# Cross-attention: the blocked values built by VectorE behind the subtraction of maxima, in place of GpSimd

## The reference

```python
ci = rms_norm(hidden_states, ln_post_cross_w)
cq = heads(ci @ cq_w, NH, CHD)                  # NH = 16 heads, CHD = 8
ck, cv = jnp.split(encoder_outputs @ ckv_w, 2, axis=-1)
ck, cv = (heads(ck, NH, CHD), heads(cv, NH, CHD))
cctx = sdpa(cq, ck, cv, causal=False)           # softmax(q k^T / sqrt(8)) v
cctx = cctx.transpose(0, 2, 1, 3).reshape(b, l, CC)
hidden_states = hidden_states + cctx @ cdense_w
```

## Time and profile before

| what | value |
|---|---|
| device time, median of 3 runs | 2231.86 us (2225.55 to 2236.3) |
| device time of the profiled execution | 2225.6 us |
| its span | 2223.8 us, 62412 instructions |
| granted TensorE clock, mean over the span | 0.967 |
| the two cross-attention phases in the span | 488.4 to 638.8 us and 1827.5 to 1977.0 us |

### The profile page before, as it was taken

The page is one execution under the profiler, slowest core; times in us unless marked ns, Lnnn a source line. Parts: engine busy times, 40 slices in busy tenths (PEclk is TensorE's granted clock), DMA queues, the critical chain, the costliest instruction groups (busy, mean ns, idle before and its releaser), DMA issues.

```text
span 2223.8 us, 62412 instructions
## 1 busy us (share of the span) xinstructions
PE 2066.6 (93%) x23424; PEld 1669.0 (75%) x23425; DVE 1368.3 (62%) x2791; ACT 1139.9 (51%) x2603; POOL 853.1 (38%) x1109
## 2 busy tenths in 40 slices
PE   7988898879979998999999979999999979979998
PEld 5656676656659997788888868897777756659997
DVE  6776776757763333666666655554788867763343
ACT  4764555438853333445444534545566637863332
POOL 1655554438942221111111112222544428952222
PEclk9999999989989998999999999999999999989999
DMA  7426877734032112200000010002444424011111
GB/s 237 122 90 140 108 118 127 104 43 111 33 99 68 57 59 72 73 2 2 2 2 2 2 42 20 19 24 92 139 134 134 126 47 124 33 49 58 58 59 34
DMA packets 122751, 159.21 MB, mean 72 GB/s; under 512 B 40867, under 2 KB 99056, under 8 KB 122384
## 3 DMA queue, kind: packets, MB, share of 16 engines
q1 hardware_dynamic: 104720, 99.59, 15.6%
q0 software_dynamic: 16560, 55.23, 11.9%
q10 hardware_dynamic: 1232, 1.05, 0.2%
HBM read 86.69 MB, written 56.28 MB: 64 GB/s over the span
## 4 chain that ended last, share of the span: by engine, by line
PE 79%; DVE 7%; issue 3%; DMA 2%; ACT 1%; POOL 1%; another core or an unknown queue 0%; POOLq 0%; DVEq 0%; ACTq 0%; SPq 0%
PE ps_all L2477 4%; PE ps_all L2479 4%; PE ps_all L2478 4%; PE ps_all L1717 3%; PE ps_all L1689 3%; PE ps_all L1242 3%; PE ps_all L1228 3%; PE ps_all L1260 3%; PE ps_all L2051 2%; PE ps_all L2502 2%; PE ps_all L2504 2%; PE ps_all L2503 2%; PE ps_all L2487 2%; PE ps_all L1703 2%; PE ps_all L1676 2%
## 5 line engine op out<-in xcount | busy, mean ns | idle before, releaser
L410 POOL TENSOR_TENSOR a_probs<-a_probs,a_sm 128x1024 f32<-128x1024 f32 x32 | 60.9, 1903 | 346.8 <-DVE a_sm L405 346.8
L1436 POOL TENSOR_TENSOR pool_w<-s_qkt,const 128x512 f32<-128x512 f32 x128 | 131.4, 1048 | 105.6 <-ACT s_qkt L1364 98.3
L2477 PE MATMUL ps_all<-f_wh,f_xh 128*128 x396 | 153.7, 388 | 5.3 <-DVE f_xl L2623 5.3
L2183 ACT ACTIVATE self_w<-ps_all,a_q_bias 128x256 f32<-128x256 f32 x128 | 53.7, 471 | 184.7 <-PE ps_all L2027 184.7
L2479 PE MATMUL ps_all<-f_wl,f_xh 128*128 x396 | 148.0, 374 | 0.0
L2478 PE MATMUL ps_all<-f_wh,f_xl 128*128 x396 | 148.0, 374 | 0.0
L2618 DVE SCALAR_TENSOR_TENSOR f_h<-ps_all,rstd,f_act_g 128x688 f32<-128x688 f32 x66 | 61.7, 934 | 135.1 <-PE ps_all L2479 135.1
L1832 POOL TENSOR_TENSOR c_kx<-kv_k,const 128x512 f32<-128x512 f32 x128 | 131.3, 1051 | 3.9 <-PE ps_all L1689 2.3
L381 DVE TENSOR_REDUCE s_mx<-ps_all 128x8 f32<-128x512 f32 x128 | 82.5, 686 | 76.4 <-PE ps_all L1228 69.1
L2541 ACT ACTIVATE f_act_g<-ps_all,rstd 128x688 f32<-128x688 f32 x66 | 55.2, 837 | 134.7 <-PE ps_all L2479 134.7
L2502 PE MATMUL ps_all<-f_dh,f_hh 128*128 x396 | 118.3, 299 | 3.9 <-DVE f_hl L2633 3.9
(11 more groups left out here) (342 smaller groups left out, 6921.6 us busy)
## 6 DMA issues: line engine op xcount, KB each, us to landing
qkv_sorted<-pool_w SPq DMA_DIRECT2D x66, 392.0 KB, 4.3
pool_w<-pool_w SPq DMA_DIRECT2D x128, 68.0 KB
s_x_in<-x_sorted SPq DMA_DIRECT2D x66, 128.0 KB
f_x_in<-x_sorted SPq DMA_DIRECT2D x66, 128.0 KB, 2.0
x_res<-x_sorted SPq DMA_DIRECT2D x66, 128.0 KB, 2.1
x_sorted<-x_res POOLq DMA_DIRECT2D x1, 4224.0 KB, 17.3
l_rows<-in_x SPq DMA_DIRECT2D x32, 128.0 KB, 2.3
x_res<-in_x SPq DMA_DIRECT2D x32, 128.0 KB, 2.9
```

The costliest lines, as they stand in the source:

```text
L1436: ins = nc.gpsimd.tensor_tensor(kx[:, p % 2, c], qkt[:, p % 2, 2 + c].rearrange("p (b k) -> p b k", b=2).unsqueeze(2) .broadcast_to([P, 2, ...
L2477: nc.tensor.matmul(bank, x_high, wh[:, w_at], start=(c == 0), stop=False)
```

## The change

`v_blocks` moves from the POOL program to the DVE program. The instruction and its waits are the same, issued on the other engine. In the DVE loop it stands behind `front(p)` and ahead of `residual(p-2)`, and it builds pair p, where GpSimd built pair p+1 in the same turn. The POOL loop keeps `spread`, `rstd_` and `put_sorted`.

```diff
                     spread(0)
                     spread(1)
-                    v_blocks(0)
                     rstd_(0)
                     for p in range(PAIRS + 3):
                         if has(p + 2):
                             spread(p + 2)
-                        if has(p + 1):
-                            v_blocks(p + 1)
                         if has(p) and p % G == G - 1 and has(p + 1):
                             rstd_(p // G + 1)
...
+                    def v_blocks(p):
+
+                        for (g0, _), c in zip(VALS, vals_in):
+                            if p == g0 * G:
+                                dve.wait_ge(c.handle, c.at(4))
+                        if pv_pe.due(p - 1):
+                            dve.wait_ge(pv_pe.handle, pv_pe.at(p - 1))
+                        nc.vector.tensor_tensor(
+                            vb[:, p % 2, :, :, :, 0:CHD].rearrange("p b j h d -> p (b j) h d"),
+                            v_all[:, p].rearrange("p b (j d) -> p (b j) d", d=CHD).unsqueeze(2)
+                            .broadcast_to([P, 2 * J, 2, CHD]),
+                            const[:, C_HALF:C_HALF + 2].unsqueeze(1).unsqueeze(3).broadcast_to([P, 2 * J, 2, CHD]),
+                            ALU.mult).then_inc(v_ok.handle, 1)
+
...
                     for p in range(PAIRS + 2):
                         if has(p):
                             front(p)
+                        if has(p):
+                            v_blocks(p)
                         if has(p - 2):
                             residual(p - 2)
```

More of the change, by code:

```diff
@@ L1836, in spread @@
                         ins.then_inc(kx_ok.handle, 1)
-                    def v_blocks(p):
-                        for (g0, _), c in zip(VALS, vals_in):
-                            if p == g0 * G:
-                                pool.wait_ge(c.handle, c.at(4))
-                        if pv_pe.due(p - 1):
-                            pool.wait_ge(pv_pe.handle, pv_pe.at(p - 1))
-                        nc.gpsimd.tensor_tensor(
-                            vb[:, p % 2, :, :, :, 0:CHD].rearrange("p b j h d -> p (b j) h d"),
-                            v_all[:, p].rearrange("p b (j d) -> p (b j) d", d=CHD).unsqueeze(2)
-                            .broadcast_to([P, 2 * J, 2, CHD]),
-                            const[:, C_HALF:C_HALF + 2].unsqueeze(1).unsqueeze(3).broadcast_to([P, 2 * J, 2, CHD]),
-                            ALU.mult).then_inc(v_ok.handle, 1)
                     def rstd_(g):
```

## The result

| | before | after |
|---|---|---|
| device time, median of 4 runs each | 2230.32 us (2225.55 to 2236.3) | 2265.64 us (2255.28 to 2271.98) |
| after / before | | 1.015, 95% interval 1.0109 to 1.0192 |
| profiled execution | 2225.6 us | 2266.34 us (span 2264.5) |
| first to last scores, cross-attention 1 and 2 | 132.96 and 132.83 us | 147.03 and 148.83 us |

The change makes the kernel slower by 35 us, 1.5%, where the prediction said +5 us and at most +16. The forecast was wrong; the slower rival (GpSimd keeps the port through both halves of a spread, 2253) was right in its mechanism and still 13 us short.

The account below looks back on a forecast made before the run. PE was taken to set the turn. Removed GpSimd work 0, undisturbed cost 0, port collisions 14 x 0.2 to 14 x 0.5 (3 to 7 us), taken as 5: 2231.9 + 5 = 2237 us, range 2228 to 2248.

Parts of the forecast that it names:

- What bounds the kernel, and the 39 us off GpSimd: Cross-attention: PE sets the turn; nobody waits for the 64 instructions leaving POOL, 39 us, worth nothing by themselves.
- Undisturbed cost 0: DVE turn: the added instruction takes 0.42 us, pushes the residual by 0.34, and costs PE nothing.
- Exclusion, and its price by `b - arrival - 0.55`: `v_blocks` against a running spread: whoever comes second waits for the other's instruction; PE pays b - arrival - 0.55, if positive.
- allowance of 0.42: DVE path to `out_t`: blocked values may be about 0.42 us late (0.16 + 0.25) before PE pays.
- The places: Group ends: blocked values arrive 0.02 us from the spreads' start; seven group ends per phase, 14 in both.
- a waiting DVE gets in between two spreads: Back-to-back spreads on GpSimd: DVE waits for one only, b = 516.01, cost 0.52 us.
- durations near 2.2: DVE durations in the changed kernel's profile: named as the sign of GpSimd keeping the port through both halves.
- VectorE is first: Tie at a group end: the spread waits 0.3, DVE nothing; 0.2 to 0.25 us in four turns, 3 us in sum.
- rival of both halves: Spreads at group ends: GpSimd keeps the port throughout, 1.53 us once in four turns, 21 us, 2253; chance 0.15.

Follow-up runs that it names:

- e1: Changed kernel with `v_blocks` on VectorE as two one-input reductions over a length-one axis, into blocks zeroed once; 2240.25 us, ratio 1.0016.
- e4: Changed kernel with the product by the mask as two `tensor_scalar` instructions of 128x128, one mask column each; 2258.0 us, before beside it 2235.6.
- e2: Changed kernel with GpSimd's indirect DMA issued ahead of the group's `rstd_` instead of behind it; 2236.09 us, ratio 1.0021.
- e3: Changed kernel with GpSimd's indirect DMA issued between the two halves of each spread; 2236.2 us, before beside it 2235.6.
- e7: Changed kernel with each half of a spread as two GpSimd instructions of 128x256; 2245.3 us, before beside it 2234.6.
- e11: Changed kernel with each spread as eight GpSimd instructions of 128x128; 2250.4 us, before beside it 2237.7.
- e9: Changed kernel with a GpSimd power of 128x4 replacing the indirect DMA issue ahead of the spread, that DMA issued behind the spread; 2266.5 us, before beside it 2237.7.
- e6: Changed kernel with a 128x1 memset on GpSimd ahead of the spread in every fourth turn; 2266.8 us, before beside it 2234.6.
- e12: e1 with three VectorE reductions of 128x512 behind `v_blocks` in every fourth turn; 2272.9 us, before beside it 2246.2.

## Why the prediction was wrong, point by point

- **What bounds the kernel, and the 39 us off GpSimd: right.** e1 takes the same 39 us off it and its turns stay at 4.25.
- **Undisturbed cost 0: right.** L1912 takes 0.41, from the rope product's 0.42. The idle time ahead of the reciprocal went down from 0.43 to 0.10 us, as forecast, and the maxima's idle of 0.42 stays:

```profile
516.52 0.41 DVE L1921 TENSOR_TENSOR x_res<-ps_all,x_res 128x256 f32<-128x256 f32 x1
517.04 0.26 DVE L1897 RECIPROCAL c_inv<-ps_all 128x16 f32<-128x16 f32 x1
```

- **Exclusion, and its price by `b - arrival - 0.55`: right.** b is the end of the GpSimd instruction that is waited for; `v_blocks` as the product of two tensors ends 0.28 to 0.29 behind it (the tensor_scalar of e4 0.10). With the b that the traces show, the formula gives for after 526.78 - 524.70 - 0.55 = 1.53 (measured 1.51), for e2 0.27 (0.24), for e3 0.45 (0.42), for e7 1.29 (1.26), for e11 1.65 (1.62). All lie within 0.03 us, so the allowance of 0.42 that is in this formula was right too.
- **The places: right.** Seven group ends a phase, 14 in all, with the asking 0.02 to 0.08 us before the spread. The turn behind loses nothing: L1912 takes 0.45 to 0.48 there, well inside the allowance.
- **The step that failed is "a waiting DVE gets in between two spreads".** From it came b = 516.01 and a cost of 0.52 us in four turns; it should have been 517.02, and the runs showed VectorE shut out through both halves, L1912 at 2.37 to 2.43 us and 1.51 to 1.56 us lost in four turns at full clock. The sign that the prediction had named for this, durations near 2.2, is what the trace shows. The row behind it, the scaling of the earlier trace rows, stood behind a spread with no DMA issue ahead of it, and the spread of the earlier trace rows follows an issue, 513.87 + 1.06 = 514.93, by 0.03. e9 shows that this is a difference, for instructions of 128x512. The prediction doubted its row for VectorE's number of elements, which isn't what mattered (e4 has as many as that row and is shut out).
- **"VectorE is first" (3 us) did not happen.** By start times VectorE was 0.02 to 0.08 us ahead of the spread in after, 0.05 to 0.11 in e6 and 0.18 to 0.24 in e9, and lost each time; in e11 it was 0.07 to 0.24 ahead eight times and won. The Trainium skill (SBUF — State Buffer, section "SBUF: two separate sides") lets the first to start have the pair for its instruction. Counted against the spread alone, the measurement says otherwise in after, e6 and e9 and agrees in e11. But VectorE asked while the DMA issue ahead of the spread was still under way, at most 0.23 us before its end, or within 0.01 us behind it. In e11 the six wins at 0.13 us ahead and more took 0.47 to 0.59 us and ended 0.37 to 0.38 behind the end of the issue, as if VectorE had waited for it. Whether the issue counts as the first to start is not shown; going by the starts of `v_blocks` and the spread alone does not price the meeting. e1 agrees with what the Trainium skill says of reductions on the same page, in its section "Who interferes with whom", that they stay clear of the pair.
- **The rival of both halves was right and under-priced.** 14 x 1.53 = 21 us is close to what was measured without the half clock, 14 x 1.55 = 22. Left out was the half clock: 4.3 and 4.4 us. The trace of before had a row for it, the wait of 1.38 us and the turn of 5.08 at the head of the phase (under e12), and the prediction put this term at nothing without naming it. 21.7 + 8.7 us, less 0.3 at the heads, are the 30.1 between first and last scores.
- **The chances and the range.** 0.15 for that rival rested on a single row that spoke against it, and the range ended below it. With one row for one side and none for the other, both ends of that question belonged inside the range.

## What to carry to other kernels

A VectorE instruction that needs the shared port is not priced by its own duration but by what it may have to wait for on GpSimd, and directly behind a DMA that GpSimd issues this can be the whole back-to-back series or most of it, not one instruction. In e11, with eighths, it was less often so. When work is moved to VectorE in such a place, use a form that stays clear of the port (a reduction over one element, e1) or keep the issue away from the front of the series (e2, e3): with e1 and e2 ten runs each could not be told from before, e3 cost 10 us by its turns. And price a wait of TensorE of the size seen here, 1.1 to 1.6 us, with what may follow it at half clock, here 40% on top; look for such a wait in the trace of before.

## What the runs showed of the hardware

- With a DMA issue on GpSimd directly ahead, its tensor instructions passed ahead of a waiting VectorE: 2 of 2 (128x512, 2.06 us) and 3 of 4 (128x256, 1.8 us) in every meeting in which it asked by 0.6 us behind their start, also where it asked up to 0.24 us before it (128x512); 6 of 8 (128x128, 2.2 us) in some, while in eight others VectorE, 0.07 to 0.24 us ahead, was first. Behind a power of the same length it got in after one.
- Two reductions of 64x128 from SBUF to SBUF took 0.27 to 0.29 us each in all 64 turns, also in the middle of a spread; a `tensor_scalar` of 128x128 with one SBUF tensor was shut out for 2.2 us like the product of two tensors.
- Near the end of a wait of TensorE of 1.1 to 1.6 us 3.4 us at half clock can begin, which cost 1.3 to 1.5 us more in after; at one such wait in after's second phase it was 10.2 us at half clock, with turns of 8.29 and 6.13.
